# First part of a two-layer gated cross-attention kernel: GpSimd takes both roots in one operation and applies both normalisations, in place of VectorE

## The chip, the cores and the metric

One core of one Trainium2 chip. The metric is device time of one execution in microseconds, median of the runs.

## The reference

Four residual updates in a row on x of shape (4, 512, 256), 2048 rows of 256, all float32:

```
x = x + tanh(g_xattn[0]) * L0_xattn(layernorm(x), ctx_1024, Wq, Wk, Wv, Wo)
x = x + tanh(g_ffn[0])   * L0_ffn(layernorm(x), w1s, w2s, w3s, W1, W2, W3, Wg)
x = x + tanh(g_xattn[1]) * L1_xattn(ctx_1024, ctx_1024, layernorm(x), ...)
x = x + tanh(g_ffn[1])   * L1_ffn(layernorm(x), ...)

def _layernorm(x, axis=-1, eps=1e-05):
    m = jnp.mean(x, axis=axis, keepdims=True)
    v = jnp.var(x, axis=axis, keepdims=True)
    return (x - m) / jnp.sqrt(v + eps)
```

L0_xattn works per row: q, k and v of one row are seen as 16 heads by 16 dimensions, scores are the 16x16 products over the heads between dimensions, softmax, and the weighted sum of v, then the output product with Wo. L0_ffn is a shared gated GELU network (256 to 1024 to 256) for every row plus one of eight experts, chosen per row by the largest logit of x @ Wg. L1_xattn is ordinary attention over 512 keys, L1_ffn a butterfly network. The change touches the two layernorms of layer 0 only.

## The kernel before

The 2048 rows are 16 tiles of 128 rows (T = 16). The program has a first part (layer 0's attention and the shared network, tile by tile), a short part that ranks the rows by expert, a part over 23 expert tiles, and layer 1. The change is in the first part.

**The first part is a pipeline of steps.** Every engine runs the same series of steps with its own instructions; in step t it works on tile t in stage 0, on tile t-1 in stage 1, and so on to tile t-4 in stage 4. The function `of(n)` gives the tile of stage n (`t0`, `t1`, ... in the code), or None at the ends. `sweep_a` writes the first six steps out, runs the next ten in a hardware loop of two steps, and writes the last one out; `drain` on each engine finishes the last tiles. The engines meet only in semaphores, and the order on each queue is the order of the code.

What one step does, by engine, with lines of the kernel before:

- **VectorE** (`step`, L1468): `scores` (L1371, product of 4096 elements a partition for tile t1, waits for `q_done`), `mult` half 0 (L1571, gated product for t4), `score_sums` (L1380), `mult` half 1, `add_attended` (L1390), `bn_stats` twice (L1395), `row_max` (L1410), `bn_aggr` twice (L1400), `shift` (L1419), epsilon added to both variances (`guarded`, L1405), `exp_sums` (L1427), then **`normal_rows` (L1437: XH, the second layernorm of tile t3, waits for `ln2_rstd`) and XN (L1507: the first layernorm of tile t0, waits for `ln1_rstd`)**, then `attended` for t2 (L1444 reciprocal, L1449 two sums of GpSimd's products, L1457 AO), and `add_shared` (L1465).
- **GpSimd** (`step`, L552): `second_root` (L514: one power of -1/2 on one element a partition, waits for `ln2_eps`), the first root (L557, waits for `ln1_eps`), then for tile t1 twice a product of 2048 elements (L576, PRODV; waits for `exp_done`, and for VectorE's `av_read` of the tile before) and an addition of 1024 (L578). In step 0 it also grows coefficients (`grown_up`, L533), in step 1 it writes a bias (`value_bias`, L544), both behind the root.
- **TensorE** (`step`, L751; `product` is L685 and `flip` is L692, whoever calls them): transpose of AO and product with Wo, second half of the shared network's up product (`up_half`, L702), k and v (WKV), the down product (`down_rows`, L733, waits for `mult_done`), transposes of XH (`normal_rows`, L741, waits for `xn2_ready`) and of XN (waits for `xn_ready`), the gate's logits, q (product with WQ, signals `q_done`), first half of the up product. In the code:

```
product(PB[2][:, 0:D], lambda k: HA[:, k, :], lambda k: W3[:, k, :], KF, s["y_done"])
...
pe.wait_ge(s["xn_ready"], n + 1)
flip(PB[1], XN[:, :], s["xT_done"])
```

- **ScalarE** copies the transposes and products out of PSUM (L1138, L1174, L1159), does both GELUs (L1129) and the exponential (L1168).
- **SyncE** stores XH to DRAM (L433, waits for `xn2_ready`) and loads the tiles of x and of the context (L410, L411).

MV holds the moments of both layernorms as (128, 2, 4): row 0 is the first layernorm, row 1 the second; columns are mean, variance, variance plus epsilon, root. MHALF is a column of -0.5.

Of the kernel before, what the change touches and what calls it, by code (L numbers as in the profile page):

```python
# [23 lines left out]
ALU = mybir.AluOpType  # L24
# [5 lines left out]
T = B * L // P  # L30
# [17 lines left out]
def spread(v, axis, n):  # L48

    shape = list(v.shape)  # L50
    shape[axis] = n
    return v.broadcast_to(shape)


def build(nc, x, ctxT, gates, wq0, wkv0, wo0, wg, wexp, wk1, wv1, wq1, wo1, bo1,
          weT, uplow, dnlow, high, cols, wc, bc, db, out):
    with ExitStack() as ctx:
        start, twins = {}, {}

        def sb(name, shape, dt=F32):  # L60
            start[name] = (nc.sbuf_base + 31) // 32 * 32
            return ctx.enter_context(nc.sbuf_tensor(name, shape, dt))
# [13 lines left out]
        def sem(name):  # L76
            return ctx.enter_context(nc.semaphore(name))
# [6 lines left out]
        X = sb("X", [P, T, D])  # L84
# [19 lines left out]
        MHALF = sb("MHALF", [P, 1])  # L104
# [19 lines left out]
        XN = sb("XN", [P, D])  # L124
        XH = sb("XH", [P, 2, D])
# [6 lines left out]
        MV = sb("MV", [P, 2, 4])  # L132
# [118 lines left out]
        xh_out = [sem("xh_out0"), sem("xh_out1")]  # L251
# [1 line left out]
        tanh_s = sem("tanh_s")  # L253

        names = """qk_prod scores rowmax shifted exp_done sums a_ready av_read ln1_stats ln1_agg ln1_eps
        ln1_rstd xn_ready ln2_stats ln2_agg ln2_eps ln2_rstd xn2_ready x1_ready xT_done xT_sb q_done
        kv_done kv_sb x2T_done x2T_sb aT_done aT_sb o_done gate_done lg_sb 
        oh_ok h1_done h2_done gelu_done mult_done y_done y_added av_prod av_half recip""".split()
        s = {n: sem(n) for n in names}
# [41 lines left out]
        c = {n: sem(n) for n in cnames}  # L301
# [15 lines left out]
        def sweep(eng, step, count, lags, start):  # L317

            def tiles(j, par, t):
                def of(n):
                    if t is not None and not 0 <= t - n < count:
                        return None
                    return lag(j, par, n)
                return of
            for t in range(2 * start):
                step(tiles(t // 2, t % 2, t))
            end = count // 2
            with eng.Fori(start, end) as j:  # L330
                step(tiles(j, 0, None))
                step(tiles(j, 1, None))
            for t in range(2 * end, count + lags):
                step(tiles(t // 2, t % 2, t))

        def sweep_a(eng, step):
            sweep(eng, step, T, 1, LAG // 2 + 1)
# [6 lines left out]
        def num(jp):  # L344
            return 2 * jp[0] + jp[1]

        def tile(n):
            return n // 2, n % 2

        def first(jp, n):  # L350
            return isinstance(jp[0], int) and num(jp) < n
# [138 lines left out]
        def _(gp):  # L490
# [17 lines left out]
            gp.iota(IOTAX[:, P + 1:P + 2 + NT], pattern=[[P, NT + 1]], base=0, channel_multiplier=0).then_inc(iotas, 1)  # L508
            gp.iota(IOTAX[:, P + 2 + NT:], pattern=[[1, T]], base=0, channel_multiplier=0).then_inc(iotas, 1)

            def second_root(n):

                gp.wait_ge(s["ln2_eps"], n + 1)
                gp.tensor_tensor(MV[:, 1, 3:4], MV[:, 1, 2:3], MHALF[:, :], ALU.pow).then_inc(s["ln2_rstd"], 1)  # L514

            done = [0]

# [32 lines left out]
                        .then_inc(bvb_ready, 1)  # L550

            def step(of):  # L552
                if (t3 := of(3)) is not None:
                    second_root(num(t3))
                if (t0 := of(0)) is not None:
                    gp.wait_ge(s["ln1_eps"], num(t0) + 1)
                    gp.tensor_tensor(MV[:, 0, 3:4], MV[:, 0, 2:3], MHALF[:, :], ALU.pow)\  # L557
                        .then_inc(s["ln1_rstd"], 1)
                    if first(t0, 1):
                        grown_up()  # L560
                    elif first(t0, 2):
                        value_bias()
                if (t1 := of(1)) is not None:
                    n, par = num(t1), t1[1]
                    gp.wait_ge(s["exp_done"], n + 1)
                    gp.wait_ge(s["kv_sb"], n + 1)
                    for hf in range(2):
                        if not first(t1, 1):

                            gp.wait_ge(s["av_read"], 2 * (n - 1) + hf + 1)  # L570
                        H2 = NH // 2
                        o = PRODV[:, :].rearrange("p (f i h j) -> p f i h j", f=2, i=DK, h=H2)[:, hf]
                        pr = spread(PR[:, par, :].rearrange("p (i o j) -> p i o j", i=DK, o=1), 2, H2)
                        v = KV[:, par, D + hf * H2 * DK:D + (hf + 1) * H2 * DK]
                        v = spread(v.rearrange("p (o h j) -> p o h j", o=1, j=DK), 1, DK)
                        gp.tensor_tensor(o, pr, v, ALU.mult).then_inc(s["av_prod"], 1)  # L576
                        gp.wait_ge(s["av_prod"], 2 * n + hf + 1)
                        gp.tensor_tensor(o[:, :, :, 0:DK // 2], o[:, :, :, 0:DK // 2], o[:, :, :, DK // 2:DK],  # L578
                                         ALU.add).then_inc(s["av_half"], 1)
                        if hf == 0 and isinstance(n, int) and n == T - 1:  # L580
                            second_root(T - 2)
                            gp.wait_ge(s["xn2_ready"], T - 1)

            sweep_a(gp, step)
            second_root(T - 1)

            def fetch(n):

# [769 lines left out]
        def _(dve):  # L1358
# [68 lines left out]
                dve.tensor_reduce(SM[:, 1, :], PR[:, t2[1], :].rearrange("p (i j) -> p i j", i=DK),  # L1427
                                  AX.X, ALU.add).then_inc(s["sums"], 1)

            def normal_rows(t3):  # L1430

                n3 = num(t3)
                dve.wait_ge(s["ln2_rstd"], n3 + 1)
                if not first(t3, 2):
                    dve.wait_ge(s["x2T_done"], n3 - 1)
                    dve.wait_ge(xh_out[t3[1]], 16 * t3[0])
                dve.tensor_scalar(XH[:, t3[1], :], X[:, n3, :], MV[:, 1, 0:1], MV[:, 1, 3:4],  # L1437
                                  ALU.subtract, ALU.mult).then_inc(s["xn2_ready"], 1)

            def attended(t2):  # L1440

                n2 = num(t2)
# [25 lines left out]
            def step(of):  # L1468
                t0, t1, t2, t3, t4 = of(0), of(1), of(2), of(3), of(4)
                if t1 is not None:  # L1470
                    scores(t1)
                if t4 is not None:
                    mult(t4, 0)
                if t1 is not None:
                    score_sums(t1)
                if t4 is not None:
                    mult(t4, 1)
                if t3 is not None:
                    add_attended(t3)
                if t0 is not None:  # L1480
                    hold(tile_in[t0[1]], 32 * t0[0] + 32)
                    stats(t0, 0, "ln1")
                if t3 is not None:
                    hold(s["x1_ready"], num(t3) + 1)
                    stats(t3, 1, "ln2")
                if t1 is not None:
                    row_max(t1)
                if t0 is not None:
                    moments(t0, 0, "ln1")
                if t3 is not None:  # L1490
                    moments(t3, 1, "ln2")
                if t1 is not None:
                    shift(t1)
                if t3 is not None:
                    guarded(t3, 1, "ln2")
                if t0 is not None:
                    guarded(t0, 0, "ln1")
                if t2 is not None:
                    exp_sums(t2)
                if t3 is not None:  # L1500
                    normal_rows(t3)
                if t0 is not None:
                    n0 = num(t0)
                    dve.wait_ge(s["ln1_rstd"], n0 + 1)
                    if not first(t0, 1):
                        dve.wait_ge(s["xT_done"], n0)
                    dve.tensor_scalar(XN[:, :], X[:, n0, :], MV[:, 0, 0:1], MV[:, 0, 3:4],  # L1507
                                      ALU.subtract, ALU.mult).then_inc(s["xn_ready"], 1)
                if t2 is not None:
                    attended(t2)  # L1510
                if t4 is not None:
                    add_shared(t4)
# [9 lines left out]
            def drain():  # L1522

                a, b, c = tile(T - 3), tile(T - 2), tile(T - 1)
                mult(a, 0)
                second_norm(b)
                exp_sums(c)
                normal_rows(b)
                mult(a, 1)
                attended(c)  # L1530
                add_shared(a)
                mult(b, 0)
                second_norm(c)
                normal_rows(c)
                mult(b, 1)
                choices()
                add_shared(b)
                places()
                mult(c, 0)
                one_hots()  # L1540
                mult(c, 1)
                expert_of_tiles()
                inverse()
                slots_of_tiles()
                add_shared(c)
# [433 lines left out]
```

## Time and profile before

| | us |
|---|---|
| median of 3 runs | 805.13 (804.56 to 805.87) |
| the profiled execution | 806.59 |
| its span, first to last instruction | 804.8 |
| first part, by the starts of the score products (L1371) | from 12.44 to 261.30 |
| mean granted TensorE clock | 0.975 of full speed |

The span and the profiled execution differ by 1.8 us, which lies outside the first and last instruction. The profile gives for each engine its busy time, for each instruction its start and length, and in square brackets the idle time of its engine before it with what ended that idle time. PE is TensorE's matrix stream, PEld its weight loads (they overlap PE), DVE VectorE, ACT ScalarE, POOL GpSimd.

### The profile page before, as it was taken

The numbers are of one execution on the slowest core, as the hardware profiler recorded it, in microseconds if no ns is written. First come the engines' busy times: TensorE is split into PE (matmuls) and PEld (weight loads), VectorE is DVE, ScalarE is ACT, GpSimd is POOL, SyncE is SP. The second block draws the span as 40 slices with busy tenths as digits, with TensorE's granted clock in tenths as the row PEclk, the third lists the DMA queues.
The fourth block names the chain that finished last, engine by engine and source line by source line (L and its number), as shares of the span: only waits on it lengthen the run. The fifth ranks groups of instructions, "written<-read, shape, count | busy, mean of one in ns | idle before, by whom it ended". The sixth has DMA issues, their size and how long they took to land.

```text
span 804.8 us, 11748 instructions
## 1 busy us (share of the span) xinstructions
PE 736.4 (92%) x4083; PEld 576.7 (72%) x4083; DVE 479.8 (60%) x818; ACT 264.0 (33%) x497; POOL 364.9 (45%) x304
## 2 busy tenths in 40 slices
PE   5759999999999898899999999999967899999996
PEld 2438878888788787466656665666556799989996
DVE  4789999999999747333111112111257767787653
ACT  1313333343334310122122212221224655466643
POOL 4788898898988842226344234432021111110000
PEclk9869999999999999899999999999998999999999
DMA  9300000100062120504045406000010101000000
GB/s 297 134 21 20 21 20 20 39 20 20 20 264 104 59 66 14 177 18 185 20 184 184 177 20 235 27 22 13 14 40 14 40 27 53 27 27 8 11 17 21
DMA packets 24285, 54.27 MB, mean 67 GB/s; under 512 B 3153, under 2 KB 20305, under 8 KB 23089
## 3 DMA queue, kind: packets, MB, share of 16 engines
q1 hardware_dynamic: 19056, 45.54, 15.7%
q0 software_dynamic: 1872, 5.11, 2.4%
q10 hardware_dynamic: 3312, 3.02, 1.1%
q8 instruction: 29, 0.48, 0.3%
q14 instruction: 16, 0.12, 0.0%
HBM read 46.45 MB, written 7.21 MB: 67 GB/s over the span
## 4 chain that ended last, share of the span: by engine, by line
PE 46%; DVE 11%; issue 5%; ACT 5%; DMA 1%; POOL 0%; ACTq 0%; DVEq 0%; POOLq 0%
PE bank L685 33%; PE bank L940 8%; PE bank L692 3%; DVE SLOT_r L1703 2%; DVE PRODV_r L1703 2%; DVE STC L1776 1%; ACT L1277 1%; ACT XS L1277 1%; DVE NM L1826 1%; ACT SLOT_r L1281 1%; DVE X L1847 1%; DVE SLOT L1844 1%; DVE X L1798 1%; DVE MVC L1778 1%; PE bank L931 1%
## 5 line engine op out<-in xcount | busy, mean ns | idle before, releaser
L685 PE MATMUL bank<-SLOT,XST 128*128 x368 | 163.9, 599 | 0.0
L576 POOL TENSOR_TENSOR PRODV<-SHARED 128x2048 f32<-128x2048 f32 x32 | 144.6, 4520 | 28.4 <-DVE bank L1449 27.9
L685 PE MATMUL bank<-SLOT,HA 128*128 (+1 forms) x624 | 142.4, 381 | 3.3 <-DVE HA L1571 2.0
L685 PEld LDWEIGHTS bank<-SLOT,HA 128*128 128x128 f32 x624 | 117.4, 190 | 37.3 <-issue 12.4
L685 PEld LDWEIGHTS bank<-SLOT,XST 128*128 128x128 f32 x368 | 68.9, 192 | 78.5 <-issue 78.4
L685 PEld LDWEIGHTS bank<-X2T,SLOT 128*128 128x128 f32 x1024 | 121.0, 194 | 1.6
L685 PE MATMUL bank<-X2T,SLOT 128*128 128x128 f32 x1024 | 121.2, 278 | 0.0
L1678 DVE TENSOR_TENSOR SHARED<-bank,G 128x512 f32<-128x512 f32 x46 | 31.8, 692 | 133.0 <-PE bank L685 133.0
L591 POOL DMA_INDIRECT XS<-normal_rows,INV x23 | 24.1, 1048 | 136.1 <-PE bank L692 115.6
L664 POOL TENSOR_TENSOR RS<-VE,MHALF 128x2 f32<-128x2 f32 x16 | 13.1, 818 | 154.2 <-DVE VE L1783 154.2
L1371 DVE TENSOR_TENSOR PRODQ<-bank,SHARED 128x4096 f32<-128x4096 f32 x16 | 70.7, 4418 | 11.2 <-PE bank L685 11.2
L578 POOL TENSOR_TENSOR PRODV<-PRODV 128x1024 f32<-128x1024 f32 x32 | 74.7, 2334 | 2.5
L1380 DVE TENSOR_REDUCE bank<-PRODQ 128x256 f32<-128x4096 f32 x16 | 70.7, 4420 | 0.1
L1669 DVE COPY HA<-bank 128x512 f32<-128x512 f32 x23 | 15.9, 692 | 71.2 <-PE bank L692 71.2
L1234 ACT ACTIVATE G<-bank 128x512 f32<-128x512 f32 x46 | 27.5, 597 | 92.9 <-PE bank L685 92.9
L940 PE MATMUL bank<-SLOT_r,PRODQ_r 128*128 128x256 f32 x256 | 47.1, 283 | 1.4 <-DVE SLOT_r L1703 1.4
L1240 ACT ACTIVATE YS<-bank 128x256 f32<-128x256 f32 x23 | 8.8, 383 | 106.1 <-PE bank L685 91.0
L940 PE MATMUL bank<-SLOT_r 128*128 128x256 f32 (+1 forms) x160 | 38.1, 312 | 4.3 <-DVE SLOT_r L1703 4.3
L940 PEld LDWEIGHTS bank<-SLOT_r,PRODQ_r 128*128 128x128 f32 x256 | 39.7, 188 | 2.3 <-DVE SLOT_r L1703 1.7
L1129 ACT ACTIVATE G<-bank 128x512 f32<-128x512 f32 x32 | 19.1, 597 | 67.1 <-PE bank L685 67.0
L1449 DVE TENSOR_REDUCE bank<-PRODV 128x128 f32<-128x1024 f32 x32 | 36.7, 1191 | 3.9 <-POOL PRODV L578 3.9
L685 PE MATMUL bank<-WKV,SHARED 128*128 128x512 f32 x64 | 32.4, 631 | 7.0 <-DMA WKV<-wkv 6.6
(232 smaller groups left out, 1301.9 us busy)
## 6 DMA issues: line engine op xcount, KB each, us to landing
SLOT<-wexp SPq DMA_DIRECT2D x9, 3072.0 KB, 11.6
expert_rows<-YS ACTq DMA_DIRECT2D x23, 128.0 KB
X<-x SPq DMA_DIRECT2D x16, 128.0 KB, 2.1
SHARED<-ctxT SPq DMA_DIRECT2D x16, 128.0 KB, 2.3
normal_rows<-XH SPq DMA_DIRECT2D x16, 128.0 KB, 1.7
WET<-ctxT SPq DMA_DIRECT2D x4, 512.0 KB, 8.2
out<-X SPq DMA_DIRECT2D x16, 128.0 KB, 1.7
WET<-weT SPq DMA_DIRECT2D x1, 1028.0 KB, 9.0
```

Source lines behind the costliest of these rows:

```text
L576: gp.tensor_tensor(o, pr, v, ALU.mult).then_inc(s["av_prod"], 1)
L578: gp.tensor_tensor(o[:, :, :, 0:DK // 2], o[:, :, :, 0:DK // 2], o[:, :, :, DK // 2:DK], ALU.add).then_inc(s["av_half"], 1)
L591: gp.indirect_dma_start(out=XS[:, n % 2, :], out_offset=None, in_=xs, in_offset=bass.IndirectOffsetOnAxis(ap=INV[:, n:n + 1], axis=0))\
L685: last = pe.matmul(dst, lhs(k), rhs(k), start=(k == 0), stop=(k == chunks - 1))
L692: last = pe.transpose(bank[:, k * P:(k + 1) * P], src[:, k * P:(k + 1) * P], IDENT[:, :])
L940: last = pe.matmul(dst, f32r(a), f32r(b), start=(k == 0 and n == 0), stop=(k == chunks - 1 and n == 2))
L1234: act.activation(G[:, hf * 512:(hf + 1) * 512], PB[1 + hf][:, :], ACT.Gelu)\
L1371: dve.tensor_tensor(PRODQ[:, :].rearrange("p (i j h) -> p i j h", i=DK, j=DK), spread(PB[1][:, 0:D].rearrange("p (i o h) -> p i o h", i=DK ...
L1380: dve.tensor_reduce(SCP.rearrange("p (i j) -> p i j", i=DK), PRODQ[:, :].rearrange("p (i j h) -> p i j h", i=DK, j=DK), AX.X, ALU.add)\
L1449: dve.tensor_reduce(aov[:, :, hf * H2:(hf + 1) * H2], PRODV[:, :].rearrange("p (f i h j) -> p f i h j", f=2, i=DK, h=H2) [:, hf, :, :, 0:D ...
L1678: dve.tensor_tensor(HB[:, t1[1], hf * 512:(hf + 1) * 512], PB[3 + hf][:, :], G[:, hf * 512:(hf + 1) * 512], ALU.mult).then_inc(e["b_mult"], 1)
L1703: dve.tensor_tensor(f32r(lo), value, rounded(high), ALU.subtract).then_inc(done, 1)
```

## The change

GpSimd takes both roots of a step in one operation over MV's two rows (`roots_a`; one row only at the ends of the pipeline) and signals a new semaphore `roots`. It waits for that itself, writes XH for tile t3 (`second_rows`) and XN for tile t0 (`first_rows`) with one operation each, and only then goes to its products. VectorE's two operations and its waits for the roots are gone. In `drain` VectorE's two remaining `normal_rows` calls go too, and GpSimd makes XH for tile 14 between its last two products and XH for tile 15 at the end. GpSimd's steps are all written out; the other engines keep the loop.

```diff
+            def roots_a(t3, t0):
+                for t, nm in ((t3, "ln2"), (t0, "ln1")):
+                    if t is not None:
+                        gp.wait_ge(s[nm + "_eps"], num(t) + 1)
+                r = slice(0, 2) if t3 is not None and t0 is not None else slice(0, 1) if t0 is not None else slice(1, 2)
+                n = r.stop - r.start
+                gp.tensor_tensor(MV[:, r, 3], MV[:, r, 2], spread(MHALF[:, :], 1, n), ALU.pow).then_inc(s["roots"], 1)
...
+            def second_rows(t3, root):
+                n3 = num(t3)
+                gp.wait_ge(s["roots"], root)
+                if not first(t3, 2):
+                    gp.wait_ge(s["x2T_done"], n3 - 1)
+                    gp.wait_ge(xh_out[t3[1]], 16 * t3[0])
+                gp.tensor_scalar(XH[:, t3[1], :], X[:, n3, :], MV[:, 1, 0:1], MV[:, 1, 3:4],
+                                 ALU.subtract, ALU.mult).then_inc(s["xn2_ready"], 1)
...
+            def first_rows(t0, root):
+                n0 = num(t0)
+                gp.wait_ge(s["roots"], root)
+                if not first(t0, 1):
+                    gp.wait_ge(s["xT_done"], n0)
+                gp.tensor_scalar(XN[:, :], X[:, n0, :], MV[:, 0, 0:1], MV[:, 0, 3:4],
+                                 ALU.subtract, ALU.mult).then_inc(s["xn_ready"], 1)
...
             def step(of):
-                if (t3 := of(3)) is not None:
-                    second_root(num(t3))
-                if (t0 := of(0)) is not None:
-                    gp.wait_ge(s["ln1_eps"], num(t0) + 1)
-                    gp.tensor_tensor(MV[:, 0, 3:4], MV[:, 0, 2:3], MHALF[:, :], ALU.pow)\
-                        .then_inc(s["ln1_rstd"], 1)
+                t0, t3 = of(0), of(3)
+                root = num(t0) + 1 if t0 is not None else num(t3) + 4
+                roots_a(t3, t0)
+                if t3 is not None:
+                    second_rows(t3, root)
+                if t0 is not None:
+                    first_rows(t0, root)
...
                         if hf == 0 and isinstance(n, int) and n == T - 1:
-                            second_root(T - 2)
-                            gp.wait_ge(s["xn2_ready"], T - 1)
-
-            sweep_a(gp, step)
-            second_root(T - 1)
+                            roots_a(tile(T - 2), None)
+                            second_rows(tile(T - 2), T + 2)
+
+            for t in range(T + 1):
+                step(lambda n: ((t - n) // 2, (t - n) % 2) if 0 <= t - n < T else None)
+            roots_a(tile(T - 1), None)
+            second_rows(tile(T - 1), T + 3)
...
-                if t3 is not None:
-                    normal_rows(t3)
-                if t0 is not None:
-                    n0 = num(t0)
-                    dve.wait_ge(s["ln1_rstd"], n0 + 1)
-                    if not first(t0, 1):
-                        dve.wait_ge(s["xT_done"], n0)
-                    dve.tensor_scalar(XN[:, :], X[:, n0, :], MV[:, 0, 0:1], MV[:, 0, 3:4],
-                                      ALU.subtract, ALU.mult).then_inc(s["xn_ready"], 1)
```

GpSimd's queue, one full step with its roots in front. Before (L514 and L557 are the two roots, L576 and L578 the products and additions):

```order
L514 TENSOR_TENSOR MV<-MV,MHALF 128x1
L557 TENSOR_TENSOR MV<-MV,MHALF 128x1
L576 TENSOR_TENSOR PRODV<-SHARED 128x2048
L578 TENSOR_TENSOR PRODV<-PRODV 128x128x8
L576 TENSOR_TENSOR PRODV<-SHARED 128x2048
L578 TENSOR_TENSOR PRODV<-PRODV 128x128x8
```

After (L518 is `roots_a`, L527 and L536 the two normalisations, L600 and L602 the products and additions):

```order
L518 TENSOR_TENSOR MV<-MV,MHALF 128x2
L527 TENSOR_SCALAR XH<-X,MV 128x256
L536 TENSOR_SCALAR XN<-X,MV 128x256
L600 TENSOR_TENSOR PRODV<-SHARED 128x2048
L602 TENSOR_TENSOR PRODV<-PRODV 128x128x8
L600 TENSOR_TENSOR PRODV<-SHARED 128x2048
L602 TENSOR_TENSOR PRODV<-PRODV 128x128x8
```

Two operations in front of the products became three, and XH and XN come ahead of the products.

VectorE's queue in the same step, from the shift to the sums of products. Before:

```order
L1419 TENSOR_TENSOR SC<-bank,SM 128x256
L1405 TENSOR_SCALAR MV<-MV 128x1 x2
L1427 TENSOR_REDUCE SM<-SHARED 128x16
L1437 TENSOR_SCALAR XH<-X,MV 128x256
L1507 TENSOR_SCALAR XN<-X,MV 128x256
L1444 RECIPROCAL RI<-SM 128x16
L1449 TENSOR_REDUCE bank<-PRODV 128x16x8 x2
```

After (the same operations bear the lines L1445, L1431, L1453, L1460 and L1465):

```order
L1445 TENSOR_TENSOR SC<-bank,SM 128x256
L1431 TENSOR_SCALAR MV<-MV 128x1 x2
L1453 TENSOR_REDUCE SM<-SHARED 128x16
L1460 RECIPROCAL RI<-SM 128x16
L1465 TENSOR_REDUCE bank<-PRODV 128x16x8 x2
```

Nothing but the two rows left; the reciprocal follows the sums directly.

## Rows read from the trace of the kernel before

**Rows 1.** The page, busy time of the engines, share of the span, instructions

```profile
PE 736.4 (92%) x4083; PEld 576.7 (72%) x4083; DVE 479.8 (60%) x818; ACT 264.0 (33%) x497; POOL 364.9 (45%) x304
```

**Rows 2.** Busy time of each engine within one step, from one score product to the next

```profile
160.94:177.66 16.72, 15.90 (x105) 13.45 (x104) 16.24 (x23) 6.00 (x10) 14.79 (x7) 1.00 0.08 24
```

**Rows 3.** Timeline of VectorE in that step (start us, length us, engine, line)

```profile
160.94 4.42 DVE L1371 TENSOR_TENSOR PRODQ<-bank,SHARED 128x4096 f32<-128x4096 f32 x1
...
170.20 0.69 DVE L1571 TENSOR_TENSOR HA<-bank,G 128x512 f32<-128x512 f32 x1
...
172.72 0.21 DVE L1405 TENSOR_SCALAR MV<-MV 128x1 f32<-128x1 f32 x2
...
173.63 0.41 DVE L1437 TENSOR_SCALAR XH<-X,MV 128x256 f32 x1 [0.38 <-POOL MV L514]
174.11 0.41 DVE L1507 TENSOR_SCALAR XN<-X,MV 128x256 f32 x1
174.44 0.25 DVE L1444 RECIPROCAL RI<-SM 128x16 f32<-128x16 f32 x1
```

**Rows 4.** Timeline of GpSimd from that step to the next roots

```profile
172.95 0.55 POOL L514 TENSOR_TENSOR MV<-MV,MHALF 128x1 f32<-128x1 f32 x1
173.47 0.61 POOL L557 TENSOR_TENSOR MV<-MV,MHALF 128x1 f32<-128x1 f32 x1
175.85 4.54 POOL L576 TENSOR_TENSOR PRODV<-SHARED 128x2048 f32<-128x2048 f32 x1 [1.77 <-DVE bank L1449]
180.47 2.33 POOL L578 TENSOR_TENSOR PRODV<-PRODV 128x1024 f32<-128x1024 f32 x1
...
189.64 0.54 POOL L514 TENSOR_TENSOR MV<-MV,MHALF 128x1 f32<-128x1 f32 x1
```

**Rows 5.** TensorE's weight loads in that step, where the down product begins

```profile
170.94 3.32 PEld L685 LDWEIGHTS bank<-SLOT,HA 128*128 128x128 f32 x16 [0.92 <-DVE HA L1571]
```

**Rows 6.** Timeline of TensorE in an earlier step, from one q product to the next

```profile
75.86 1.11 PE L685 MATMUL bank<-WQ,XT 128*128 128x256 f32 x4
...
87.06 0.19 PEld L685 LDWEIGHTS bank<-SLOT,HA 128*128 128x128 f32 x1 [0.24 <-DVE HA L1571]
...
90.73 0.36 PEld L692 LDWEIGHTS bank<-IDENT,XH 128*128 128x128 f32 x2
91.05 0.25 PEld L692 LDWEIGHTS bank<-IDENT,XN 128*128 128x128 f32 x2
...
92.26 1.11 PE L685 MATMUL bank<-WQ,XT 128*128 128x256 f32 x4
```

**Rows 7.** Timeline of VectorE, score products of tiles 4 and 15

```profile
77.00 4.42 DVE L1371 TENSOR_TENSOR PRODQ<-bank,SHARED 128x4096 f32<-128x4096 f32 x1
...
261.30 4.41 DVE L1371 TENSOR_TENSOR PRODQ<-bank,SHARED 128x4096 f32<-128x4096 f32 x1
```

**Rows 8.** GpSimd operations of later parts: shortest, median, longest ns; a group with mean ns

```profile
L664 POOL TENSOR_TENSOR RS<-VE,MHALF x16: 688/696/1085, 601.3 to 781.1; 128x2 f32<-128x2 f32 x16
...
L618 POOL TENSOR_SCALAR TMPH<-PRODV,HIC x32: 468/476/982, 356.4 to 417.8; 128x256 f32<-128x256 f32 x32
...
L620 POOL TENSOR_TENSOR PRODV<-TMPH 128x256 f32<-128x256 f32 x8 | 5.1, 638 | 0.7
```

**Rows 9.** Timeline of GpSimd and VectorE in step 2

```profile
37.57 0.56 POOL L557 TENSOR_TENSOR MV<-MV,MHALF 128x1 f32<-128x1 f32 x1
38.17 0.41 DVE L1507 TENSOR_SCALAR XN<-X,MV 128x256 f32<-128x256 f32 x1 [1.18 <-POOL MV L557]
...
41.91 4.42 DVE L1371 TENSOR_TENSOR PRODQ<-bank,SHARED 128x4096 f32<-128x4096 f32 x1 [0.50 <-PE bank L685]
```

**Rows 10.** The last tiles: chain of work, then timelines of VectorE and TensorE

```profile
271.29 3.72 PE bank L685 x16
...
297.68 0.41 DVE L1437 TENSOR_SCALAR XH<-X,MV 128x256 f32<-128x256 f32 x1 [0.66 <-POOL MV L514]
...
299.03 0.38 PE L692 MATMUL bank<-IDENT,XH 128*128 128x128 f32 x2
```

More of the change, by code:

```diff
@@ L255, in build @@
         names = """qk_prod scores rowmax shifted exp_done sums a_ready av_read ln1_stats ln1_agg ln1_eps
-        ln1_rstd xn_ready ln2_stats ln2_agg ln2_eps ln2_rstd xn2_ready x1_ready xT_done xT_sb q_done
+        roots xn_ready ln2_stats ln2_agg ln2_eps xn2_ready x1_ready xT_done xT_sb q_done
         kv_done kv_sb x2T_done x2T_sb aT_done aT_sb o_done gate_done lg_sb
@@ L509, in _ @@
             gp.iota(IOTAX[:, P + 2 + NT:], pattern=[[1, T]], base=0, channel_multiplier=0).then_inc(iotas, 1)
-            def second_root(n):
-                gp.wait_ge(s["ln2_eps"], n + 1)
-                gp.tensor_tensor(MV[:, 1, 3:4], MV[:, 1, 2:3], MHALF[:, :], ALU.pow).then_inc(s["ln2_rstd"], 1)
+            def roots_a(t3, t0):
[20 more added lines that the diff above has]
+                                 ALU.subtract, ALU.mult).then_inc(s["xn_ready"], 1)
             done = [0]
@@ L1428, in exp_sums @@
                                   AX.X, ALU.add).then_inc(s["sums"], 1)
[L1430 to L1438, printed above, removed]
             def attended(t2):
@@ L1527, in drain @@
                 exp_sums(c)
-                normal_rows(b)
                 mult(a, 1)
@@ L1533, in drain @@
                 second_norm(c)
-                normal_rows(c)
                 mult(b, 1)
```

## The prediction

> **What bounds the kernel now.** I read the page first. TensorE is busy for 92% of the span, far ahead of the others [rows 1]. That is a mean over parts with different limits, and the change lies in the first part alone, so the next view is the busy time within one step there: 16.72 us long, VectorE busy for 16.24, TensorE 15.90, GpSimd 14.79 [rows 2]. Three engines are nearly full, and the question is which ring of waits sets the step.
>
> VectorE's timeline gives it. Its step is full but for 0.38 us before XH, which waits for GpSimd's root [rows 3]. GpSimd waits 1.77 us for VectorE's sum before its first product, and is back at its next root 13.79 us after that product's start (175.85 to 189.64), just as VectorE has added epsilon [rows 4]. So VectorE and GpSimd hold one another at 16.7 us a step. TensorE waits in that ring too, at one place: the down product's weights wait 0.92 us for `mult` half 1 [rows 5]. The reader should see how little of that 0.92 TensorE can get back. The earlier step of [rows 6] shows TensorE nearly unhindered, with a gap of only 0.24 us before those weights, and its period, from one q product to the next, is 92.26 - 75.86 = **16.40 us**. From the score product of tile 4 to that of tile 15 the kernel takes 261.30 - 77.00 = 184.30 us, 11 steps of **16.75** [rows 7]. TensorE's own floor is thus 0.35 us under the present step.
>
> **What the change takes from VectorE.** VectorE was idle from 173.25 (XH's 173.63 less the wait of 0.38), and an operation of 0.41 lets the next one start 0.33 after its own start (174.11 to 174.44 [rows 3]), 0.08 before its end. Without the two rows the reciprocal could start at 173.17 and not at 174.44: **1.27 us a step**, the wait and both rows with the gap between them. VectorE's ring falls to 16.72 - 1.27 = 15.45 us. Over 11 steps that would be 14 us, if nothing else held the step.
>
> **What it adds to GpSimd.** The two roots (0.52 from start to start and 0.61 [rows 4]) become one over two elements. The nearest row is the same operation on 128x2 in the last part: 0.69 at best, 0.70 median, 1.09 at worst [rows 8]. I take the median; layout differs a little. A row of 256 elements with one tensor input has its nearest row in L618, the same operation and size: 0.47 at best, 0.48 median, 0.98 at worst [rows 8]. Both rows together: 0.95 us. The upper end for an undisturbed one is the operation with two tensor inputs, 0.64 [rows 8]; the lower end is 0.41, VectorE's own time. The wait for its own semaphore costs about 0.08 (175.85 + 4.54 = 180.39, next start 180.47 [rows 4]), and I take as much for the wait on VectorE's epsilon.
>
> GpSimd's own ring: 13.79 + 0.70 + 0.08 + 0.95 = 15.5 us. Its products can start as soon as XN is written, since VectorE's sum comes 1.27 us earlier. GpSimd does not become the bound; 0.9 us is left to TensorE's floor.
>
> **Where XH and XN come in time.** This is what the result hangs on, since TensorE now waits for GpSimd and not for VectorE. I count from Q, the end of a q product. In [rows 6] that is 75.86 + 1.11 = 76.97. The score product starts 0.03 us later [rows 7]. Epsilon is done at 172.93, 11.99 after the score product's start [rows 3]. Then 0.08 for the wait, 0.70 root, 0.08 own wait, 0.48 XH, 0.47 XN, 0.05 to TensorE. XH is seen at Q + 0.03 + 11.99 + 0.08 + 0.70 + 0.08 + 0.48 + 0.05 = Q + 13.41, XN at Q + 13.88. TensorE, unhindered, loads for the transposes at 90.73 and 91.05, Q + 13.76 and Q + 14.08 [rows 6]. XH has 0.35 us to spare, XN 0.20. The transposes don't wait. The other need, `mult` half 1, ends 170.20 + 0.69 - 160.94 = 9.95 after the score product [rows 3], Q + 9.98, and the weights are wanted at 87.06, Q + 10.09 [rows 6]. So the ring is TensorE's: each q product releases the score product, and a step is **16.40 us**.
>
> **The ends of the pipeline.** In step 2 GpSimd is late and XN is on the path: root from 37.57, XN from 38.17 to 38.58, score product at 41.91 once q is there [rows 9]. Now step 1's XN stands in front of GpSimd's bias and products, so the root comes about 0.5 us later, and GpSimd's row adds 0.1 to 0.2 us over VectorE's. Score product 2 comes some 0.6 us later. Step 3 gives that back: GpSimd starts its products behind XN and not behind VectorE's sum, and one root operation replaces two. I cost steps 0 to 3 at nothing, bounds -0.7 and +0.7 us. In the last tiles, from 271.29 on, the chain runs over TensorE [rows 10]. The last XH ends at 298.09 and its transpose starts at 299.03, so GpSimd's dearer row (0.1 us) is hidden by the up product; without it the whole tail would come 0.1 us later. XH's stores and SyncE's loads behind them move by 0.1 us at most and the loads serve a later step. GpSimd's written-out steps take away loop branches, costed at nothing: no row shows a branch's time, and GpSimd's 0.9 us to spare would cover it. The parts behind only shift.
>
> **The sum.** 11 steps from 16.75 to 16.40: 184.30 - 180.40 = **3.9 us less**. The profiled execution took 806.59 (span 804.8, 1.8 around it), so 802.7; that execution stands 1.5 us above the median of 805.13, and against the median it is **801.2**.
>
> **The rivals.** With R for the root and W for both rows, XN's lateness is R + W - 1.85 (the 1.65 taken above and the 0.20 to spare), and the step is 16.40 plus that, where it is positive.
>
> *XN comes too late, and the gain is gone.* Were a row twice as dear on GpSimd as on VectorE, 2 x 0.41 [rows 3], W would be 1.64, R + W = 2.34, the lateness 0.49, the step 16.89 and the time 11 x 0.14 = 1.5 us above now: 806.6. With W at the two-input price, 1.28, and R = 0.70 the lateness is 0.13 and 2.4 us are still gained. Between R + W = 2.05 and 2.35 lies no measurable difference (a measurement here tells from no change about 0.2%, 1.6 us): 803.5 to 806.7. For it: a root over two elements has taken 1.09, which alone makes R + W 2.04. Against it: the one row that fits in operation and size, L618, has a median of 0.48 and not 0.82 [rows 8]. Chance 0.17. The Trainium skill (GPSIMD Engine Reference, section 4.1 Engine selection) speaks against such a move: elementwise work belongs on VectorE, GpSimd is about twice as slow with two inputs, with one input roughly at line rate. By the first half of that rule it would be the 806.6 of this rival, by the second half my sum; L618 has one input and agrees with the second.
>
> *Slower: VectorE holds GpSimd up.* In L618 an operation took up to 0.98 and not 0.48 [rows 8]. Were both rows held up like that in each step, by VectorE's sums beside them, R + W = 0.70 + 1.96 = 2.66, the lateness 0.81, the step 17.21, and the time 11 x 0.46 = 5.1 us more: 810.2. It decides from R + W = 2.35 on. For it: the second root, with VectorE's XH beside it, took 0.61 and the first 0.55 [rows 3, 4]. Against it: XH and XN leave VectorE, and of what then stands beside GpSimd's rows the sums of products (L1449, behind the reciprocal) stand beside its product from 175.85 on today, which keeps its 4.54 [rows 4]. Chance 0.08. The Trainium skill (SBUF — State Buffer, section Who interferes with whom) has the two engines share a port pair under an exclusive lock, which VectorE takes for tensor_scalar in a two-port mode or with two SBUF inputs. By that rule the lock would leave with XH and XN and this rival would not come; the 0.61 beside XH agrees.
>
> *VectorE's whole 1.27 us is gained.* Then TensorE's 16.40 is no floor, and the time would be near 791. [Rows 6] speak against it. Chance 0.02.
>
> That GpSimd would not do what the change says has no support: its queue holds the operations in the new order. It is counted in the first rival.
>
> **The numbers.** The forecast has 0.73. Faster by over 0.2%: 0.73 + 0.02 = 0.75; within 0.2%: 0.17; slower: 0.08. The forecast's own range is 801.2 with -0.7 for the first steps and -0.6 for the scatter of the runs, and up to 803.3 if XN is late by 0.15 to 0.2. To leave out no more than 2 in 10 I go into the first rival: 799.9 to 804.6.
>
> **What would show it.** Right: score products from tile 4 on 16.40 us apart, each with a short wait for TensorE (about 0.9 us on VectorE); the down product's weights with a gap of 0.24 us and not 0.92; transposes of XH and XN with no wait for GpSimd; root about 0.70, rows 0.48; GpSimd idle about 0.9 us before its root. Wrong: a wait of TensorE for XN by GpSimd in each step, roots of 1.09 or rows over 0.64, a step above 16.6, or a new wait elsewhere on TensorE that brings its period above 16.40; also a first score product of tile 4 later than 77.7.

## The result and the profile after

The changed kernel takes **818.11 us** (median of 4 runs, 816.8 to 820.38) against 805.5 (4 runs), a ratio of **1.0155** with a 95% interval of 1.0125 to 1.0184. The forecast was 801.2; the change costs 12.6 us. The profiled execution has a span of 818.5 us against 804.8.

The view that tells most is the timeline of one step of the kernel after. DVE is VectorE, POOL is GpSimd, PEld and PE are TensorE's weight loads and products; columns as in [rows 3].

```profile
150.52 4.42 DVE L1397 TENSOR_TENSOR PRODQ<-bank,SHARED 128x4096 f32<-128x4096 f32 x1 [1.85 <-PE bank L711]
...
160.57 0.19 PEld L711 LDWEIGHTS bank<-SLOT,HA 128*128 128x128 f32 x1 [0.24 <-DVE HA L1576]
...
162.22 0.21 DVE L1431 TENSOR_SCALAR MV<-MV 128x1 f32<-128x1 f32 x2
...
162.57 0.71 POOL L518 TENSOR_TENSOR MV<-MV,MHALF 128x2 f32<-128x2 f32 x1 [0.38 <-DVE MV L1431]
...
163.39 1.23 POOL L527 TENSOR_SCALAR XH<-X,MV 128x256 f32<-128x256 f32 x1
164.59 1.22 POOL L536 TENSOR_SCALAR XN<-X,MV 128x256 f32<-128x256 f32 x1
...
164.66 0.20 PEld L718 LDWEIGHTS bank<-IDENT,XH 128*128 128x128 f32 x2 [0.45 <-POOL XH L527]
...
165.87 0.20 PEld L718 LDWEIGHTS bank<-IDENT,XN 128*128 128x128 f32 x2 [1.00 <-POOL XN L536]
...
166.04 0.53 PEld L711 LDWEIGHTS bank<-WG,X2T 128*128 128x128 f32 x4
...
166.35 0.38 ACT L1200 ACTIVATE XT<-bank 128x256 f32<-128x256 f32 x1 [0.82 <-PE bank L718]
...
166.78 1.13 PE L711 MATMUL bank<-WQ,XT 128*128 128x256 f32 x4
...
167.95 4.42 DVE L1397 TENSOR_TENSOR PRODQ<-bank,SHARED 128x4096 f32<-128x4096 f32 x1 [1.85 <-PE bank L711]
```

The root takes 0.71 and is where the prediction put it. **Each row takes 1.22 to 1.23 us**, not 0.48. TensorE waits 0.45 us for XH and 1.00 for XN; VectorE waits 1.85 us for the q product. The down product's weights, which waited 0.92 us in [rows 5], come after a gap of 0.24, as in [rows 6]: that wait did go, and a longer one took its place on the same engine, at the transposes. The ring of the step now runs through GpSimd: score product at 150.52, epsilon done at 162.43 (162.22 + 0.21), root, XH, XN, the transpose at 165.87, the q product at 166.78, the next score product at 167.95. GpSimd itself still waits 0.38 us for epsilon, so it is late rather than full.

The score products of tiles 4 and 15 in the same view, to be set beside [rows 7]:

```profile
80.63 4.42 DVE L1397 TENSOR_TENSOR PRODQ<-bank,SHARED 128x4096 f32<-128x4096 f32 x1 [1.87 <-PE bank L711]
...
272.79 4.42 DVE L1397 TENSOR_TENSOR PRODQ<-bank,SHARED 128x4096 f32<-128x4096 f32 x1 [1.85 <-PE bank L711]
```

192.16 us for 11 steps, **17.47 a step** where before had 16.75: 7.9 us of the loss. The busy time of one step, beside [rows 2], shows VectorE relieved (15.60 for 16.24) and GpSimd filled up (16.80 for 14.79). Behind the window and its length stand PE, PEld, DVE, ACT and POOL, then TensorE's granted clock as a share of full speed (1.00 in both kernels' steps, so the clock has no part in this), the DMA share and GB/s:

```profile
167.95:185.47 17.52, 16.02 (x104) 13.53 (x103) 15.60 (x20) 6.10 (x10) 16.80 (x8) 1.00 0.07 22
```

The rest of the 13.7 us between the two profiled executions lies at the ends. From the first score product to that of tile 4 it is 80.63 - 12.61 = 68.02 us after and 77.00 - 12.44 = 64.56 before, 3.5 us more; behind tile 15's it is 818.5 - 272.79 = 545.7 and 804.8 - 261.30 = 543.5, 2.2 us more. Three operations of the same group in the early steps show that the price of a row does not hang on what stands beside it: at 5.18 and 23.43 VectorE does nothing, at 39.73 its sums of products run (from 38.57, 2.29 long).

```profile
5.18 1.23 POOL L536 TENSOR_SCALAR XN<-X,MV 128x256 f32<-128x256 f32 x1
...
23.43 1.22 POOL L536 TENSOR_SCALAR XN<-X,MV 128x256 f32<-128x256 f32 x1
...
39.73 1.22 POOL L536 TENSOR_SCALAR XN<-X,MV 128x256 f32<-128x256 f32 x1
```

Of the tail's 2.2 us, 0.7 comes before the weights of the last XH: from tile 15's score product to them it is 311.07 - 272.79 = 38.28 us after, 298.92 - 261.30 = 37.62 before, and 37.64 in e2, e6 and e7, where XH's row is quick. TensorE waits there for the XH of tile 13:

```profile
286.58 0.20 PEld L718 LDWEIGHTS bank<-IDENT,XH 128*128 128x128 f32 x2 [0.48 <-POOL XH L527]
```

The other 1.5 us lies behind the last XH: 507.4 us after and 505.9 before, where the other runs have 503.3 to 506.9.

### The profile page after: what moved, and what is told of

The parts are those of the page before. It is cut to its first block, busy times and chain, and to the rows that moved or that the text cites. A ratio compares the mean times of both kernels' runs of the same rounds, so it can differ in the third digit from the quotient of the medians.

```text
span 818.5 us, 11666 instructions
## 1 busy us (share of the span) xinstructions
PE 736.7 (90%) x4083; PEld 575.5 (70%) x4083; DVE 468.4 (57%) x786; ACT 265.5 (32%) x497; POOL 399.0 (49%) x323
## 4 chain that ended last, share of the span: by engine, by line
PE 49%; DVE 19%; POOL 12%; issue 11%; ACT 5%; DMA 3%; SPq 0%; DVEq 0%; POOLq 0%; ACTq 0%
PE bank L711 36%; PE bank L966 8%; DVE bank L1406 5%; PE bank L718 4%; POOL PRODV L600 3%; POOL XN L536 2%; POOL XH L527 2%; DVE SLOT_r L1708 2%; POOL PRODV L602 2%; DVE PRODV_r L1708 1%; POOL MV L518 1%; DVE STC L1781 1%; DMA XS<-normal_rows,INV 1%; ACT L1303 1%; DVE PRODQ L1397 1%
## 5 line engine op out<-in xcount | busy, mean ns | idle before, releaser
L600 POOL TENSOR_TENSOR PRODV<-SHARED 128x2048 f32<-128x2048 f32 x32 | 144.5, 4516 | 0.0
L711 PEld LDWEIGHTS bank<-SLOT,HA 128*128 128x128 f32 x624 | 119.3, 192 | 33.3 <-issue 14.8
L602 POOL TENSOR_TENSOR PRODV<-PRODV 128x1024 f32<-128x1024 f32 x32 | 74.8, 2339 | 2.5
L683 POOL DMA_INDIRECT SLOT<-expert_rows,POS x16 | 15.8, 988 | 49.6 <-DMA expert_rows<-YS 45.9
L1465 DVE TENSOR_REDUCE bank<-PRODV 128x128 f32<-128x1024 f32 x32 | 36.8, 1194 | 4.7 <-POOL PRODV L602 4.7
```

The lines of the kernel that those rows point to most:

```text
L711: last = pe.matmul(dst, lhs(k), rhs(k), start=(k == 0), stop=(k == chunks - 1))
L1465: dve.tensor_reduce(aov[:, :, hf * H2:(hf + 1) * H2], PRODV[:, :].rearrange("p (f i h j) -> p f i h j", f=2, i=DK, h=H2) [:, hf, :, :, 0:D ...
```

## The experiments

All ran on one core, each compared with the kernel before on the same chip; e1 and e5 ran once, since they are read for the durations of single operations. The question after the result: why does GpSimd take 1.23 us for a row that looks like one of 0.48, and is that all? The row the prediction had leaned on, L618, multiplies by one column and by the immediate 1.0; the changed kernel's subtracts a column and multiplies by another. Three things differ or could: the number of columns, the arithmetic, and VectorE's work beside it.

### e1_forms: ten operations in an idle stretch

```diff
...
+            Xa, Pa, Pb = X[:, 0, :], MV[:, 1, 0:1], MV[:, 1, 3:4]
...
+            for width, p0, p1, o0, o1 in PROBES:
+                settle()
+                run(gp.tensor_scalar(TMP[:, 0:width], X[:, 0:2, :].rearrange("p t d -> p (t d)")[:, 0:width],
+                                     (Pa if p0 else 0.5), (Pb if p1 else 1.0), ...))
+            settle()
             gp.wait_ge(z_first, 6 * 4)
```

> The kernel before with ten GpSimd tensor_scalar operations in a stretch where GpSimd waits anyway (between the last early fetch and the first-stage wait of the part over the expert tiles), from X into the scratch tile TMPH, with a wait for its own semaphore between them: one or two scalars taken from a column, operations multiply, subtract, add, widths 128, 256, 512. Nothing of the result is touched. Theory A (the form: two scalars from columns instead of one column and an immediate): all operations with two columns take about 1.22 us at 256 whatever the arithmetic, all with one column and an immediate about 0.47. Theory B (subtract instead of multiply): subtract then multiply is dear with a column and an immediate too, multiply twice with two columns is cheap at 0.47. Theory C (VectorE beside it holds GpSimd up): the two-column form is cheap here, 0.5, since VectorE hardly works in this stretch; against it, the first row of the changed kernel took 1.23 with VectorE idle. Time of the kernel as before within 0.2%.

Measured: 805.37 us beside 804.86. The operations in order are: multiply by a column and by 1.0; subtract a column, multiply by a column; subtract a column, multiply by 1.0; multiply by two columns; multiply by a column, add a column; multiply by a column, add 1.0; then subtract and multiply with two columns at 128 and at 512; multiply twice at 512; subtract and multiply with immediates alone. GpSimd's timeline:

```profile
336.83 0.49 POOL L643 TENSOR_SCALAR TMPH<-X,MV 128x256 f32<-128x256 f32 x1
337.42 1.23 POOL L643 TENSOR_SCALAR TMPH<-X,MV 128x256 f32<-128x256 f32 x1
338.75 1.15 POOL L643 TENSOR_SCALAR TMPH<-X,MV 128x256 f32<-128x256 f32 x1
340.00 0.55 POOL L643 TENSOR_SCALAR TMPH<-X,MV 128x256 f32<-128x256 f32 x1
340.65 0.55 POOL L643 TENSOR_SCALAR TMPH<-X,MV 128x256 f32<-128x256 f32 x1
341.30 0.48 POOL L643 TENSOR_SCALAR TMPH<-X,MV 128x256 f32<-128x256 f32 x1
341.88 0.80 POOL L643 TENSOR_SCALAR TMPH<-X,MV 128x128 f32<-128x128 f32 x1
342.77 2.16 POOL L643 TENSOR_SCALAR TMPH<-X,MV 128x512 f32<-128x512 f32 x1
345.03 0.79 POOL L643 TENSOR_SCALAR TMPH<-X,MV 128x512 f32<-128x512 f32 x1
345.91 1.07 POOL L643 TENSOR_SCALAR TMPH<-X 128x256 f32<-128x256 f32 x1
```

The second column costs 0.06 to 0.08 us whatever the arithmetic. Subtracting and not multiplying costs 0.68 with two columns (1.23 for 0.55) and 0.66 with one (1.15 for 0.49); with immediates alone the operation still takes 1.07. Theory A falls, theory B stands, and theory C falls with the 1.23 at 337.42: VectorE does nothing beside it, from 336.68 to 339.25. By width, subtract and multiply grows from 0.80 through 1.23 to 2.16, some 3.5 ns an element of a partition; multiply twice from 0.49 at 256 to 0.79 at 512, 1.2 ns.

### e2_one_scalar: both rows in the quick form

```diff
-                gp.tensor_scalar(XH[:, t3[1], :], X[:, n3, :], MV[:, 1, 0:1], MV[:, 1, 3:4],
-                                 ALU.subtract, ALU.mult)
+                gp.tensor_scalar(XH[:, t3[1], :], X[:, n3, :], MV[:, 1, 3:4], 1.0,
+                                 ALU.mult, ALU.mult)
```

and the same in XN.

> The changed kernel with both GpSimd rows in the form of one column and an immediate: x times root times 1.0. The mean is not subtracted in either layernorm; nothing else differs. If the ring argument of the prediction holds and only the price of the row was wrong: rows 0.47 us, step 16.40, score products 4 to 15 in about 180.4 us, time about 3.9 us under before, ratio 0.995. Rival (GpSimd in the path costs more than its operations: late signals, another wait on TensorE): rows 0.47 but a step above 16.6. If VectorE beside it is what slows the rows (Theory C), rows stay near 1.2 and the step near 17.5.

Measured: 802.46 us against 804.86, ratio **0.997** (0.9953 to 0.9988). The rows take 0.48 on average. VectorE's score products of tiles 4 to 6:

```profile
76.05 4.42 DVE L1397 TENSOR_TENSOR PRODQ<-bank,SHARED 128x4096 f32<-128x4096 f32 x1 [1.06 <-PE bank L711]
92.46 4.42 DVE L1397 TENSOR_TENSOR PRODQ<-bank,SHARED 128x4096 f32<-128x4096 f32 x1 [0.83 <-PE bank L711]
108.86 4.42 DVE L1397 TENSOR_TENSOR PRODQ<-bank,SHARED 128x4096 f32<-128x4096 f32 x1 [0.74 <-PE bank L711]
```

That of tile 15 starts at 256.52: (256.52 - 76.05) / 11 = **16.41 us a step**, where the prediction had 16.40. GpSimd is idle for 0.75 to 0.93 us before its root in the steps from tile 6 on, as forecast (0.9). So the ring of the prediction was right, and the row's price is what broke it. The whole-kernel gain of 2.4 us is smaller than the 3.9 forecast, which lies just outside the interval (0.9953 is 3.8 us); single runs of this kernel spread from 799.4 to 805.2.

### e3_xn_gpsimd: XH back on VectorE, XN on GpSimd

```diff
-                    second_rows(t3, root)                  # GpSimd
...
+                    normal_rows(t3)                        # VectorE, waits for roots
```

> The changed kernel with XH given back to VectorE (waits for the joint root); only XN on GpSimd. Form theory: XN is seen by TensorE 14.2 us after the score product, near TensorE's own 14.1, VectorE's ring is about 16.3: step 16.4 to 16.6, time 1.5 to 4 us under before. Port theory (VectorE's row and GpSimd's row start together when the root is done and one holds the other for its whole length): either XH takes or waits about 1.2 us and VectorE's ring rises to 17.3, or XN starts 0.3 to 0.4 us later and the step is about 16.8, time as before.

Measured: 805.44 us against 804.86, ratio 1.0007 (0.9991 to 1.0023), no difference; the step is (262.15 - 79.57) / 11 = 16.60. Two neighbouring steps:

```profile
142.15 1.37 POOL L536 TENSOR_SCALAR XN<-X,MV 128x256 f32<-128x256 f32 x1
142.18 0.41 DVE L1460 TENSOR_SCALAR XH<-X,MV 128x256 f32 x1 [0.66 <-POOL MV L518]
...
158.64 1.22 POOL L536 TENSOR_SCALAR XN<-X,MV 128x256 f32<-128x256 f32 x1
158.75 0.58 DVE L1460 TENSOR_SCALAR XH<-X,MV 128x256 f32 x1 [0.81 <-POOL MV L518]
```

Started 0.03 us apart, XN takes 0.15 us more; started 0.11 behind it, XH takes 0.17 more. The two get in each other's way, by less than a fifth of a microsecond. VectorE's XH is not held for the 1.22 us of GpSimd's row: it ends at 159.33, and XN at 159.86. The Trainium skill (SBUF — State Buffer, section Who interferes with whom) says that beside a VectorE operation in a two-port mode whoever issues second fully blocks until the first has finished, and that one with a single SBUF input outside these modes does not contend with GpSimd at all. No run shows in which mode XH ran; this trace agrees with neither for these two operations, and the measurement decides. The step comes out at the top of the form theory's range (16.4 to 16.6) and under the port theory's (16.8), but the whole time came out as the port theory had it, as before, and not 1.5 to 4 us under it. TensorE's wait moved behind XN (0.66 us in the first of these steps), and VectorE, with XH's wait for the longer joint root, is full again.

### e4_roots_only: both rows back on VectorE

```diff
-                    second_rows(t3, root)                  # GpSimd, and first_rows
...
+                dve.wait_ge(s["roots"], n3 + 4)            # VectorE's rows as before, n0 + 1 for XN
```

> The changed kernel with both rows given back to VectorE: only the joint root (and GpSimd's written-out steps) are left of the change. Theory: XH waits for a root of 0.71 over two elements where it waited for one of 0.55, and XN follows at once; step 16.75 to 16.85, time within 0.3% of before. If instead the joint root or the written-out steps caused the loss: step towards 17.4 and 12 us more.

Measured: 807.28 us against 804.86, ratio 1.0028 (1.0017 to 1.0038). The step is (263.51 - 78.35) / 11 = 16.83, inside the expected band. One root of 0.70 over two elements is dearer for XH than one of 0.55: in the steps from tile 6 on XH waits 0.65 to 0.81 us where it mostly waited 0.37 to 0.67, and the joint root saves VectorE little, as XN had waited only in every second step (0.15 us: it started 0.48 behind XH at 173.63, and 0.33 behind it in the next step). Alone, this part of the change is a small loss. The steps account for 11 x 0.08 = 0.9 us of it. In the profiled execution 1.7 us more arise at one down product of the tail, 5.41 us long where [rows 10] has 3.72: TensorE had waited 1.91 us before it, and its granted clock is at the lower of its two levels, 0.50 of full speed, from 275 to 278 us. The same product before had waited 1.78 and ran at 1.00. Whether the other executions had that is not shown. That the written-out steps take part in it was not tried apart.

### e5_forms2: which operation is the dear one

The same edit with other operations: add then multiply with two columns; add a column, multiply by 1.0; multiply then subtract; subtract then multiply; add a column, add 1.0; then `tensor_tensor` of two 256-wide inputs with add, subtract, multiply, and one of 2 elements. The time was 805.58 us beside 805.52.

> A second set of GpSimd operations in the same idle stretch. Found so far: at width 256, subtract then multiply took 1.23 us with two columns and 1.15 with one, 1.07 with none, while multiply twice and multiply-add took 0.55 with two columns and 0.48 with one. Theory (subtraction as such is the slow operation of tensor_scalar on GpSimd): add then multiply with two columns 0.55, with one 0.48, add twice 0.48; multiply then subtract near 1.2; subtract then multiply 1.23 again. Rival (only the pairs that begin with multiply are quick): add then multiply near 1.2 too, multiply then subtract 0.55. For tensor_tensor of two 256-wide inputs, which is served by another routine: 0.64 for add, subtract and multiply alike.

```profile
337.88 0.55 POOL L641 TENSOR_SCALAR TMPH<-X,MV 128x256 f32<-128x256 f32 x1
338.52 0.48 POOL L641 TENSOR_SCALAR TMPH<-X,MV 128x256 f32<-128x256 f32 x1
339.11 1.24 POOL L641 TENSOR_SCALAR TMPH<-X,MV 128x256 f32<-128x256 f32 x1
340.45 1.23 POOL L641 TENSOR_SCALAR TMPH<-X,MV 128x256 f32<-128x256 f32 x1
341.77 1.15 POOL L641 TENSOR_SCALAR TMPH<-X,MV 128x256 f32<-128x256 f32 x1
343.01 0.73 POOL L646 TENSOR_TENSOR TMPH<-X 128x256 f32<-128x256 f32 x1
343.82 0.73 POOL L646 TENSOR_TENSOR TMPH<-X 128x256 f32<-128x256 f32 x1
344.62 0.73 POOL L646 TENSOR_TENSOR TMPH<-X 128x256 f32<-128x256 f32 x1
```

Add then multiply with two columns takes 0.55, and the computed result of a row can have that form. Multiply then subtract takes 1.24. Both are against the rival, that only pairs beginning with multiply are quick. But **add twice takes 1.15**, where the theory said 0.48: a miss. So it is not subtraction alone. Of the pairs tried, multiply-multiply, multiply-add and add-multiply are quick, and subtract-multiply, multiply-subtract and add-add are slow. A quick path for some pairs fits that, a slow operation does not; which other pairs are in it was not tried, and why these are slow stays open. `tensor_tensor` knows no such difference, and with both inputs from X it takes 0.73, more than the 0.64 of [rows 8].

### e6_one_dear_row: a dose between

Only XH in the form of e2; XN still subtracts.

> The changed kernel with the cheap form in XH only (no mean subtracted in the second layernorm), XN still subtract and multiply. A dose between the changed kernel and the one with two cheap rows. The prediction's formula with R 0.71 and W 0.48 + 1.22: lateness 2.41 - 1.85 = 0.56, step 16.96. The changed kernel came out at 17.47 where the formula gives 17.7, since with XN late its copy no longer queues behind XH's on ScalarE; so 16.75 to 16.96, time 0 to 2.5 us above before. If the loss were not XN's lateness but GpSimd's total work, the step would be half way, 16.9 to 17.0, as well; if it were XH's lateness alone, 16.41.

Measured: 807.64 us against 805.52, ratio 1.0022 (1.0004 to 1.0039). The step is (263.05 - 79.03) / 11 = 16.73, just under the expected band (16.75 to 16.96), and neither the 16.9 to 17.0 of GpSimd's total work nor the 16.41 of XH's lateness alone. The time is 2.1 us over before although the step is not: from the first score product to that of tile 4 it is 79.03 - 12.29 = 66.74 us where before has 64.56. A step with XH at 0.48 and XN at 1.22:

```profile
176.07 1.22 POOL L536 TENSOR_SCALAR XN<-X,MV 128x256 f32<-128x256 f32 x1
176.37 0.36 PEld L718 LDWEIGHTS bank<-IDENT,XH 128*128 128x128 f32 x2
...
177.34 0.20 PEld L718 LDWEIGHTS bank<-IDENT,XN 128*128 128x128 f32 x2 [0.61 <-POOL XN L536]
```

XH is in time, XN is late by 0.61. With two dear rows the step is 17.47, with one 16.73, with none 16.41: the second dear row costs its full 0.74, the first only 0.32, since it first eats up the 0.42 us that XN had to spare.

### e7_minus_mean: the same result by an addition

```diff
-        MV = sb("MV", [P, 2, 4])
+        MV = sb("MV", [P, 2, 5])
...
+            def minus_mean(r, nm):
+                dve.tensor_scalar(MV[:, r, 4:5], MV[:, r, 0:1], -1.0, None, ALU.mult).then_inc(negated[nm], 1)
...
+                gp.wait_ge(negated["ln2"], n3 + 1)
...
-                gp.tensor_scalar(XH[:, t3[1], :], X[:, n3, :], MV[:, 1, 0:1], MV[:, 1, 3:4],
-                                 ALU.subtract, ALU.mult)
+                gp.tensor_scalar(XH[:, t3[1], :], X[:, n3, :], MV[:, 1, 4:5], MV[:, 1, 3:4],
+                                 ALU.add, ALU.mult)
```

with `minus_mean` behind `guarded` on VectorE, and the same in XN.

> The changed kernel computing the same with an addition: VectorE writes minus the mean into a fifth column of MV behind the epsilon operations (two operations on one element), GpSimd's rows add that and multiply by the root. If add then multiply costs 0.55: R + W = 0.71 + 1.08 = 1.79, lateness below nothing, step 16.4 to 16.45, score products 4 to 15 in 180.4 to 181 us, time 2 to 4 us under before, the first version that beats it. If add is as dear as subtract: 17.5 and 12 us above.

Measured: **802.14 us** against 805.52, ratio **0.9962** (0.9942 to 0.9983). It beats both kernels. The step is (259.49 - 79.02) / 11 = 16.41. The same place of the step as in the first timeline:

```profile
206.00 0.70 POOL L519 TENSOR_TENSOR MV<-MV,MHALF 128x2 f32<-128x2 f32 x1 [0.82 <-DVE MV L1434]
...
206.80 0.56 POOL L529 TENSOR_SCALAR XH<-X,MV 128x256 f32<-128x256 f32 x1
...
207.34 0.56 POOL L539 TENSOR_SCALAR XN<-X,MV 128x256 f32<-128x256 f32 x1
...
207.58 0.36 PEld L721 LDWEIGHTS bank<-IDENT,XH 128*128 128x128 f32 x2
...
207.95 0.21 PEld L721 LDWEIGHTS bank<-IDENT,XN 128*128 128x128 f32 x2
...
208.50 0.38 ACT L1203 ACTIVATE XT<-bank 128x256 f32<-128x256 f32 x1
208.65 0.52 PEld L714 LDWEIGHTS bank<-WG,X2T 128*128 128x128 f32 x4 [0.49 <-ACT X2T L1167]
...
209.09 0.73 PEld L714 LDWEIGHTS bank<-WQ,XT 128*128 128x128 f32 x4
...
210.27 4.42 DVE L1400 TENSOR_TENSOR PRODQ<-bank,SHARED 128x4096 f32<-128x4096 f32 x1 [0.62 <-PE bank L714]
```

No weight load waits for GpSimd, and VectorE waits 0.62 us for TensorE, with room for its two extra operations.

## Why the prediction was wrong

- **The step that failed** is in "What it adds to GpSimd": "A row of 256 elements with one tensor input has its nearest row in L618, the same operation and size ... Both rows together: 0.95 us. The upper end for an undisturbed one is the operation with two tensor inputs, 0.64". It was not the same operation: subtract-multiply instead of multiply-multiply. Both rows took 2.45 us. The upper end was wrong for the same reason; it took one price of `tensor_scalar` for the price of every pair of operations.
- **The size of W apart, the ring held.** The root was 0.71 (forecast 0.70), the reciprocal moved up, the down product's wait went, TensorE's own period was 16.41 in e2 and e7 (forecast 16.40), GpSimd was idle 0.75 to 0.93 us before its root in e2 (forecast 0.9) and 0.59 to 0.82 in e7, whose rows take 0.56. With the measured R + W = 0.71 + 2.45 = 3.16 the lateness formula gives 1.31 and a step of 17.71; it was 17.47, and with one dear row 16.73 where it gives 16.96. The 1.85 in that formula was too small by this 0.23 to 0.24 us, because a late XN no longer shares the way with XH: from XN's weight load to the next score product the kernel after takes 167.95 - 165.87 = 2.08 us, e7 210.27 - 207.95 = 2.32. Most of the difference is on TensorE. In e7 q's weights (209.09) stand behind those of the gate's logits (208.65), which wait for XH's copy, and follow the start of XN's copy by 0.59; in the kernel after the logits' weights are in at 166.04, and q's follow the copy by 0.43. The copy itself comes 0.55 after XN's weight load in e7 and 0.48 in the kernel after.
- **The ends.** Steps 0 to 3 were costed at nothing with bounds of 0.7, and the tail at nothing. The early steps cost 3.5 us: the four intervals between the first five score products grow by 1.20, 1.00, 0.64 and 0.62, as both operations of GpSimd are on the path, and in step 2 XN ends at 40.95 where VectorE's ended at 38.58 [rows 9]. In e7, with rows of 0.56, the same stretch takes 79.02 - 14.28 = 64.74, as before, so this is the same wrong price. TensorE's granted clock is not behind it: its mean over this stretch is 0.81 before, 0.82 after and 0.82 in e7. Of the tail's 2.2 us, the 0.7 up to the last XH has the same cause, at the XH of tile 13; the last one, which the prediction looked at, is indeed hidden. The other 1.5 us stays open.
- **The rivals.** The slower rival had the right mechanism and place, "It decides from R + W = 2.35 on", and the wrong cause, VectorE holding GpSimd up; the first row of the kernel, with VectorE idle, took 1.23 as well. The rival that priced a row by VectorE's time twice (1.64 for both) came nearer than the forecast, also for another reason. The Trainium skill (GPSIMD Engine Reference, section 4.1 Engine selection), whose first half the prediction priced in the first rival and whose second half it read in favour of its sum, speaks of operations with one input at roughly line rate; the quick pairs agree with it, 1.2 ns an element beside the 1.08 of VectorE's score product (4.42 us for 4096), and the slow ones, also with one input, do not, 3.5 ns. In the slower rival the prediction took the second root's 0.61 beside XH for agreement with the lock that the Trainium skill describes (SBUF — State Buffer, section Who interferes with whom). Its rows don't bear that out: root and XH overlap (173.47 and 173.63), XH keeps its 0.41, and neither waits for the other's end.

## What to carry to other kernels

A duration stands for an operation only where the arithmetic is the same too, not just the name of the instruction, the shape and the engine; before work moves to another engine, time that exact form in an idle stretch. When a stall is removed from a ring, work out for each operation that is moved how much time it has to spare at the engine that waits for it next: here XN had 0.42 us by e2 and e6, and all that it took beyond that came out in the step, one for one. On GpSimd write a layernorm's row as (x + (-mean)) * root; in e7 that took 0.56 us for 1.23.

## What the runs showed of the hardware that was not expected

- GpSimd's `tensor_scalar` on 256 elements a partition has two prices: 0.48 to 0.55 us for multiply-multiply, multiply-add and add-multiply, 1.07 to 1.24 us for subtract-multiply, multiply-subtract and add-add. Its `tensor_tensor` takes 0.73 for add, subtract and multiply alike.
- VectorE's row and GpSimd's row in the same step slow one another, GpSimd's by 0.15 us or VectorE's by 0.17, and neither waits for the other's end (e3).
- The first score product starts anywhere from 12.05 to 14.28 us in these profiles, and from 12.44 to 13.40 in before, e1 and e5, which run the same code up to there. How much of the scatter of some microseconds a run comes from it is not shown, but it lies outside the steps, which is why the step is the better measure of a change of this size.
